# Attention stage of a fused layer kernel: the two layer-norm roots move from GpSimd into VectorE's Newton chain

## What is computed

```python
x = x + layernorm(attention(layernorm(x)))     # this stage; x is 32 x 256 x 128, fp32
# layernorm(x) = (x - mean) / sqrt(var + 1e-5), over the last axis
# attention:  Q, K = normalised 4-wide heads of xn @ Wq.T, xn @ Wk.T  (16 heads)
#             Qn = normalize(Q @ W_nudge);  V = xn @ Wv.T (64 per head)
#             scores = Qn.K * scale + k_bonus(K);  causal softmax;  out = P.V @ Wout.T
x = x + layernorm(ffn(layernorm(x)))           # later stages, not touched by the change
x = x + layernorm(recurrence(layernorm(x)))
x = x + layernorm(mixture_of_experts(layernorm(x)))
```

## Time and profile before

| | |
|---|---|
| median of 3 runs (lowest, highest) | 1899.07 us (1897.19, 1900.87) |
| the profiled execution | 1898.16 us, span 1896.4 us, mean granted TensorE clock 0.961 |
| PE busy over the span | 1695.4 us, 89% |
| PEld / DVE / ACT / POOL busy | 1240.9 / 1331.5 / 886.4 / 999.0 us (65 / 70 / 47 / 53%) |
| instructions | 43410 |
| the attention stage | from 0 to about 864 us of the span |

### The profile page before, as it was taken

How to read it: one execution, slowest core, us unless ns; L and a number is a source line. 1 busy time by engine, 2 the same in 40 slices (tenths; PEclk the granted TensorE clock), 3 DMA queues, 4 the chain that set the end, 5 groups by cost and what they waited for, 6 DMA issues and landing times. The chain is left out here.

```text
span 1896.4 us, 43410 instructions
## 1 busy us (share of the span) xinstructions
PE 1695.4 (89%) x12768; PEld 1240.9 (65%) x12768; DVE 1331.5 (70%) x4113; ACT 886.4 (47%) x1955; POOL 999.0 (53%) x1825
## 2 busy tenths in 40 slices
PE   4999999999999999975999999999999997568885
PEld 2666666666666666654778888888878885335553
DVE  6777777777777777753456777777777676457775
ACT  2655565555555555532344444444444442123332
POOL 6777766777777767742222333333333332137776
PEclk8999999999999999988999999999999998679997
DMA  1011111111110111201011000000010005034431
GB/s 39 10 52 40 36 50 50 50 50 50 50 44 31 50 50 50 78 12 39 12 56 56 29 29 29 29 32 31 31 36 32 27 23 196 33 109 121 127 115 36
DMA packets 78236, 95.72 MB, mean 50 GB/s; under 512 B 7046, under 2 KB 62995, under 8 KB 78160
## 3 DMA queue, kind: packets, MB, share of 16 engines
q1 hardware_dynamic: 70992, 77.91, 13.0%
q0 software_dynamic: 7168, 16.87, 2.5%
HBM read 53.14 MB, written 43.69 MB: 51 GB/s over the span
## 5 line engine op out<-in xcount | busy, mean ns | idle before, releaser
L648 ACT ACTIVATE wgu<-score 128x384 f32<-128x384 f32 x512 | 223.1, 489 | 99.8 <-PE score L472 94.5
L317 POOL TENSOR_SCALAR_AFFINE_SELECT wgu<-wgu 128x512 f32<-128x512 f32 x256 | 163.9, 640 | 155.1 <-ACT wgu L648 146.3
L1239 PE MATMUL main<-hT_high,h_high 128*128 128x512 f32 x512 | 223.5, 436 | 0.9 <-ACT hT_high L1448 0.9
L1241 PE MATMUL main<-hT_high,h_low 128*128 128x512 f32 x512 | 203.5, 398 | 0.0
L495 PE MATMUL outp<-wgu 128*64 128x256 f32 (+1 forms) x2048 | 197.8, 336 | 0.9 <-POOL wgu L317 0.9
L495 PEld LDWEIGHTS outp<-wgu 128*64 128x64 f32 x2048 | 128.5, 138 | 58.7 <-issue 17.8
L1248 PE MATMUL main<-hT_low,h_high 128*128 128x512 f32 x512 | 139.1, 393 | 0.1
L529 PE MATMUL back<-wout,wgu 128*128 128x128 f32 x1024 | 131.3, 282 | 0.0
L790 DVE TENSOR_TENSOR wgu<-spread,wgu 128x512 f32<-128x512 f32 x128 | 87.0, 680 | 61.9 <-PE spread L515 56.8
L1694 DVE SCALAR_TENSOR_TENSOR th<-th,main 128x512 f32<-128x512 f32 x64 | 43.9, 686 | 122.9 <-ACT th L1479 122.9
L1380 PE MATMUL main<-wgu,xgT 128*128 x192 | 106.0, 634 | 23.4 <-DVE xgT L1738 16.0
(11 more groups left out here) (270 smaller groups left out, 4205.3 us busy)
## 6 DMA issues: line engine op xcount, KB each, us to landing
sorted_d<-row_buf SPq DMA_DIRECT2D x26, 772.0 KB, 3.7
xg<-sorted_d SPq DMA_DIRECT2D x48, 386.0 KB, 3.2
wgu<-in_gate_up SPq DMA_DIRECT2D x4, 2048.0 KB, 9.0
xa<-in_x SPq DMA_DIRECT2D x32, 128.0 KB, 3.5
xr<-in_x SPq DMA_DIRECT2D x32, 128.0 KB, 3.2
x_d<-x SPq DMA_DIRECT2D x32, 128.0 KB, 1.9
x1c<-x_d SPq DMA_DIRECT2D x16, 256.0 KB, 2.8
x1v<-x_d SPq DMA_DIRECT2D x16, 256.0 KB, 2.7
```

The lines of the kernel that those rows point to most:

```text
L317: pool.affine_select(out=blocks, in_=blocks, compare_op=ALU.is_ge, fill=0.0, base=0, pattern=[[0, 4], [1, P]], channel_multiplier=-1).then ...
L648: act.activation(prob[:, h // 2 % (RING // 2), :, h % 2, :], score[h % BANKS][:, 0:SC].rearrange("p (c q) -> p c q", q=P), ACT.Exp).then_i ...
L1239: pe.matmul(main[m % 2][:, :], w[0][:, k, m * P:(m + 1) * P], src[0][:, k, :], start=(k == 0), stop=False)
L1241: pe.matmul(main[m % 2][:, :], w[1][:, k, m * P:(m + 1) * P], src[0][:, k, :], start=False, stop=False)
```

## The change

The GpSimd function `rstd` and its tiles are taken out. The tiles of the short Newton chain (ssg2, r2, nt2, nu2) grow from 32 to 36 columns; the last four hold the variances (two row tiles, for y and m) plus epsilon, times 0.25. A new DVE function `roots` waits for both sets of means and variances, writes these columns with one `tensor_scalar`, waits for that, and runs the chain, which gave the norm of the rotated q only and stood at the start of the next step. It is now at the end of the step, behind ssg2, and runs in each step that has an entry y or m, so in 37 steps where there were 32. `xn` is computed straight behind it, and `yn` and `x1` behind xn. In the PE step the wait for `rec` stands between the weighted values and the row totals of the first quarter and no longer ahead of both. The factor 0.25 with the chain's last factor 0.25 in place of 0.5 gives 1/sqrt(var + epsilon).

```diff
@@ -116,13 +116,10 @@
         back_row = sb("back_row", [P, HEADS])
         low_row = sb("low_row", [P, HEADS])
         low_sel = sb("low_sel", [P, 1])
-        pow_half = sb("pow_half", [P, 2, TT])
 
         xa = sb("xa", [P, TT, D])
         stat_a = sb("stat_a", [P, TT, 6])
         mv_ya = sb("mv_ya", [P, 2, TT, 2])
-        ve_ya = sb("ve_ya", [P, 2, TT])
-        rstd_ya = sb("rstd_ya", [P, 2, TT])
         xn = sb("xn", [P, TT, D])
         xnT = [sb(f"xnT{i}", [P, T]) for i in range(2)]
         sq1 = sb("sq1", [P, TT * 2 * HEADS, DH])
@@ -135,10 +132,11 @@
         qkT = sb("qkT", [P, T])
         sq2 = sb("sq2", [P, TT, HEADS, DH])
         ss2 = sb("ss2", [P, TT, HEADS])
-        ssg2 = sb("ssg2", [P, TT, HEADS])
-        r2 = [sb(f"r2_{i}", [P, TT, HEADS]) for i in range(4)]
-        nt2 = sb("nt2", [P, TT, HEADS])
-        nu2 = sb("nu2", [P, TT, HEADS])
+        NQ = TT * HEADS
+        ssg2 = sb("ssg2", [P, NQ + 2 * TT])
+        r2 = [sb(f"r2_{i}", [P, NQ + 2 * TT]) for i in range(4)]
+        nt2 = sb("nt2", [P, NQ + 2 * TT])
+        nu2 = sb("nu2", [P, NQ + 2 * TT])
         qraw = sb("qraw", [P, TT, HEADS, DH])
         ek = sb("ek", [P, TT, HEADS, DH])
         ek1 = sb("ek1", [P, TT, HEADS, DH])
@@ -282,7 +280,7 @@
             const(pool.memset(ident[:], 0.0))
             const(pool.affine_select(out=ident[:], in_=ident[:], compare_op=ALU.not_equal, fill=1.0, base=0,
                                      pattern=[[-1, P]], channel_multiplier=1))
-            const(pool.memset(pow_half[:], -0.5))
+            const(pool.memset(ssg2[:], 1.0))
             const(pool.tensor_copy(ident_b[:], ident[:]))
 
             def late_constants():
@@ -332,18 +330,6 @@
                         c += 1
                         wait_apart(pool, s[name], STEPS_K * n + c, s["const"])
                         v = rest[k + (2 if name == "qsplit" else 0)][:]
-
-            def rstd(y, m):
-
-                n = m if m is not None else y + 5
-                if y is not None:
-                    wait_apart(pool, s["mv_y"], TT * (y + 1), s["const"])
-                if m is not None:
-                    wait_apart(pool, s["mv_a"], TT * (m + 1), s["const"])
-                h = slice(0 if y is not None else 1, 2 if m is not None else 1)
-                pool.tensor_scalar(ve_ya[:, h], mv_ya[:, h, :, 1], 1.0, EPS, ALU.mult, ALU.add).then_inc(s["ve"], 1)
-                wait_apart(pool, s["ve"], n + 1, s["const"])
-                pool.tensor_tensor(rstd_ya[:, h], ve_ya[:, h], pow_half[:, h], ALU.pow).then_inc(s["rstd"], 1)
 
             def bonus(n, between):
 
@@ -444,8 +430,6 @@
                                            1.0, 0.0, ALU.mult, ALU.add)
                     pool.tensor_scalar(q_aug[:, :, 24:27], qp[:, :, :, DH], 1.0, 0.0,
                                        ALU.mult, ALU.add).then_inc(s["qaug"], 1)
-                if y is not None or m is not None:
-                    rstd(y, m)
                 mask(b, 7)
 
             rounds(pool, step)
@@ -480,7 +464,6 @@
                     return
                 if g == 0:
                     wait(pe, s["val"], 4 * (b + 1))
-                    wait(pe, s["rec"], b)
                 wait(pe, s["masked"], PAIRS_A * b + 2 * g + 2)
                 wait(pe, s["raw"], GROUPS * b + g)
 
@@ -496,6 +479,8 @@
                                           weights(h, k), start=(k == 0), stop=(k == 1),
                                           tile_position=(0, DV * i), skip_group_check=True)
                 m.then_inc(s["p_out"], 1)
+                if g == 0:
+                    wait(pe, s["rec"], b)
                 for k in range(2):
                     for j in range(GH):
                         m = pe.matmul(total[AUG * j:AUG * (j + 1), k * P:T], pick[:, g, :],
@@ -751,6 +736,19 @@
                     did(dve.scalar_tensor_tensor(out=r[k + 1][:], in0=nu[:], scalar=3 * w, in1=r[k][:],
                                                  op0=ALU.add, op1=ALU.mult))
 
+            def roots(y, m):
+
+                c = m if m is not None else y + 5
+                if y is not None:
+                    dve.wait_ge(s["mv_y"], TT * (y + 1))
+                if m is not None:
+                    dve.wait_ge(s["mv_a"], TT * (m + 1))
+                h = slice(0 if y is not None else 1, 2 if m is not None else 1)
+                both = ssg2[:, NQ:NQ + 2 * TT].rearrange("p (h i) -> p h i", h=2)
+                dve.tensor_scalar(both[:, h], mv_ya[:, h, :, 1], EPS, 0.25, ALU.add, ALU.mult).then_inc(s["ve"], 1)
+                dve.wait_ge(s["ve"], c + 1)
+                rsqrt(ssg2, r2, nt2, nu2, "rsq2", c, 0.25)
+
             def constants():
                 dve.wait_ge(s["w"], 96)
                 dve.tensor_copy(wv_part[0][:], wv[:]).then_inc(s["wv_split"], 1)
@@ -801,11 +799,10 @@
 
             def step(b, f, n, m, z, y, par):
                 if f is not None:
-                    rsqrt(ssg2, r2, nt2, nu2, "rsq2", f, 0.25)
                     wait(dve, s["qsplit"], STEPS_K * f)
                     wait(dve, s["qraw"], f + 1)
                     dve.tensor_tensor(q5[:, :, :, 0:DH], qraw[:],
-                                      r2[3][:].rearrange("p i (h o) -> p i h o", o=1)
+                                      r2[3][:, 0:NQ].rearrange("p (i h o) -> p i h o", i=TT, o=1)
                                       .to_broadcast([P, TT, HEADS, DH]), ALU.mult).then_inc(s["q4"], 1)
                 reciprocal(z)
                 last = isinstance(b, int) and b == B - 1
@@ -876,25 +873,25 @@
                     dve.wait_ge(s["ek1"], n + 1)
                     dve.reciprocal(sg[:], ek1[:]).then_inc(s["sg"], 1)
                     dve.wait_ge(s["ss2"], n + 1)
-                    dve.tensor_scalar(ssg2[:], ss2[:], NORM_MIN2, None, ALU.max).then_inc(s["ssg2"], 1)
+                    dve.tensor_scalar(ssg2[:, 0:NQ], ss2[:].rearrange("p i h -> p (i h)"), NORM_MIN2, None,
+                                      ALU.max).then_inc(s["ssg2"], 1)
                     dve.wait_ge(s["ssg2"], n + 1)
+                roots(y, m)
+                if m is not None:
+                    wait(dve, s["p_xnT"], m)
+                    for i in range(TT):
+                        mm = dve.tensor_scalar(xn[:, i, :], xa[:, i, :], mv_ya[:, 1, i, 0:1],
+                                               r2[3][:, NQ + TT + i:NQ + TT + i + 1], ALU.subtract, ALU.mult)
+                    mm.then_inc(s["xn"], 1)
                 if y is not None:
-                    wait(dve, s["rstd"], y + 6)
                     for i in range(TT):
                         mm = dve.tensor_scalar(yn[:, i, :], y_sb[:, i * D:(i + 1) * D], mv_ya[:, 0, i, 0:1],
-                                               rstd_ya[:, 0, i:i + 1], ALU.subtract, ALU.mult)
+                                               r2[3][:, NQ + i:NQ + i + 1], ALU.subtract, ALU.mult)
                     mm.then_inc(s["yn"], 1)
                     dve.wait_ge(s["yn"], y + 1)
                     wait(dve, s["xr"], 16 * (y + 1))
                     wait(dve, s["x1_out"], 16 * y)
                     dve.tensor_tensor(x1[:], yn[:], xr[:], ALU.add).then_inc(s["x1"], 1)
-                if m is not None:
-                    wait(dve, s["rstd"], m + 1)
-                    wait(dve, s["p_xnT"], m)
-                    for i in range(TT):
-                        mm = dve.tensor_scalar(xn[:, i, :], xa[:, i, :], mv_ya[:, 1, i, 0:1],
-                                               rstd_ya[:, 1, i:i + 1], ALU.subtract, ALU.mult)
-                    mm.then_inc(s["xn"], 1)
 
             rounds(dve, step)
 
```

More of the change, by code:

```diff
@@ L190, in attention_layer @@
         back = ps("back", [P, 512])
-        names = ("w", "const", "xa", "stat_a", "mv_a", "ve", "rstd", "xn", "p_xnT", "xnT", "p_qk", "sq1", "ss1",
+        names = ("w", "const", "xa", "stat_a", "mv_a", "ve", "xn", "p_xnT", "xnT", "p_qk", "sq1", "ss1",
                  "ssg1", "rsq1", "qkn", "p_qkT", "qkT", "p_rot", "sq2", "ek", "qraw", "ss2", "ssg2", "rsq2", "ek1",
```

## The result

The changed kernel takes 1907.1 us (median of 8 runs, 1902.51 to 1911.98), the kernel before in the same comparison 1899.05 (8 runs, 1897.14 to 1901.65): ratio 1.0041, 95% interval 1.0024 to 1.0058. The change costs 8 us. The forecast was 1898.6 with a range up to 1907.0, so it was too low by 8.5, and the median lies 0.1 above the range. The profiled execution took 1906.67 us (span 1904.9) against 1898.16 (span 1896.4).

What follows compares the result with a forecast made beforehand. PE was taken as the bound, waiting 0.88 us a step for xn. Loop -5.4 and pipeline ends +4.9 gave -0.5: 1897.7 from the profiled 1898.16, and 1898.6 as the median 0.9 above; range 1885 to 1907.

Steps and rivals of the forecast that it cites:

- The bound and what one step is worth: Attention loop: PE is the bound; its transpose of xn waits 0.88 us a step, 23.8 in 27 steps, the most recoverable.
- The walk through POOL's rows: DVE's chain beside POOL's instructions in the loop: 3.6 us long, xn earlier by 0.2 us a step, -5.4 in 27 steps.
- the xn pair: xn's two DVE instructions behind the chain in the loop: with POOL idle they take 0.60 us and not 1.00.
- ACT's copy held by yn: Loop: ACT's y_sb copy waits 1.4 us for yn; POOL's 1.44 us wait covers it: nothing, at most 0.3 a step.
- The ends: Both ends of the pipeline, where the chain is dearer than POOL's power: +4.9 us, bounds +3 and +7.
- (a) to (c): Pipeline start: second xn net +1.9 us, third xn about +0.7, PE's start behind ssg2 in the third step +0.65.
- The first xn: Start of the pipeline: the first root (entry 0) is hidden by the weights' load, so it costs nothing.
- (e): Pipeline's end: the last yn waits 2.7 us for its root, hidden by nothing, where it waited 1.09 for POOL: +1.6.
- The sum: Loop -5.4 and ends +4.9 make -0.5 us, so 1898.6; own range 1892 to 1905, chance 0.48.
- its own undoing: Prediction is wrong if POOL's instructions stand elsewhere in the step than put, or the ends cost more than 7 us.
- B: Rival: POOL holds the loop's chain throughout, 3.92 us; +1 to +12, with the ends 1905 to 1916; chance 0.20.
- C: Rival: ACT's copy waiting for yn becomes the new wait, delaying masks 0.3 us a step, +8, about 1907; chance 0.07.

## Why the prediction was wrong

- **The bound and what one step is worth: right.** PE's 0.88 a step was the most to be had, and with POOL waiting nearly all of it came: 0.8 us were left of 23.8.
- **The walk through POOL's rows: right.** Chain 3.6 forecast, 3.54 measured; held by the mask and both bonus instructions, as put; the xn pair 0.60 forecast, 0.60 measured. The fourth instruction passed the copy of k. The gain per step came out at 0.30 and not 0.2, since xn follows the chain by 0.03 and not by 0.15 and the chain is 0.06 shorter. -8.1 in place of -5.4, inside its bounds.
- **ACT's copy held by yn: right in kind, cost not quite nothing.** ACT waits 1.57 (forecast 1.4), and the cover of 1.44 at POOL is used up: PE waits 0.10 a step for masks, inside the bound of 0.3. It is why PE's wait fell by 0.43 and the step only by 0.30.
- **The ends: priced too low at the start.** The run with POOL's power there agrees with the 4.9 (4 to 6 measured), but even that run is 1.8 us behind before when the loop begins. In the changed kernel's own trace the pipeline's fill costs 6.6 where (a) to (c) made 3.3, and with the last root the ends cost 8.0, above the upper bound of 7: PE waits for the second xn 7.12 and not 3.35, for the third 0.81 and the fourth 1.29 where before had none:

```profile
27.31 0.69 PE L549 MATMUL front<-ident,xn 128*128 128x128 f32 x2 [7.12 <-DVE xn L883]
...
43.86 0.69 PE L549 MATMUL front<-ident,xn 128*128 128x128 f32 x2 [0.81 <-DVE xn L883]
...
66.52 0.69 PE L549 MATMUL front<-ident,xn 128*128 128x128 f32 x2 [1.29 <-DVE xn L883]
```

  The first xn, put at nothing, is 2.2 us later too (8.32 against 6.16), though that is down to 1.0 at the matmuls behind it. At the other end (e) was right: ACT's last y_sb is 1.90 earlier (856.59 against 858.49) and yn 0.46, so the root costs 1.4 (forecast 1.6).
- **The sum: right for what it summed, and in part by luck.** 6.6 at the start, -8.1 in the loop, -0.4 in the unrolled steps behind it and 1.4 for the last root make -0.5 at the last yn, which is what the trace shows (-0.46). The forecast has the same -0.5 because two misses cancel: the ends 3.1 dearer, the loop 2.7 better and 0.4 behind it. With the loop at its old place the changed kernel runs at 0.9992 of before (0.9983 to 1.0001), and -0.5 us is 0.9997.
- **The step that failed: the sum stops where the attention stage stops, and all code behind it was put at nothing without a reason.** It counts what each instruction costs where it runs, and not what 67 more of them do to the place of the code behind. That term is +8, more than all others leave together. Of what the prediction named as its own undoing, POOL stands in the step where it was put; the ends did come out above 7, but the loop paid for that. Nor was it one of the rivals: B's and C's times cover 1907 by chance, and the traces show 0.45 a step left and 0.10 for the masks.
- **The clock at the start of the next stage** is a small second term, not forecast. In the windows of 880 to 885 us before stands at a granted clock of 1.00 and the kernel after at 0.50:

```profile
880.00:885.00 5.00, 1.87 (x7) 1.25 (x8) 3.61 (x6) 1.57 (x3) 0.00 (x0) 1.00 0.00 0
```

```profile
880.00:885.00 5.00, 2.97 (x7) 1.86 (x7) 2.91 (x6) 1.21 (x2) 0.00 (x0) 0.50 0.00 0
```

  PE had no work from 860 to 870 in both. The rise comes some 11 us later after the change, and PE goes from 1.3 us ahead (872) to 0.6 behind (886), in the profiled run. Between runs of the changed kernel this varies: those with a mean clock of 0.962 took 1902.5 to 1903.9, those at 0.955 took 1910.3 to 1912.0. The loop's 8 us stand in the profiled runs beside it, so the two add.

## What to carry to other kernels

This is shown for one loop of one engine. When a change adds or removes instructions on an engine ahead of a hardware loop, look in the new trace at idle time without a releaser on the loop's first instruction, and at instruction packets in its passes; if both are new, put a few dozen instructions more ahead of it before judging the change. The price of this chain of small DVE instructions on the critical path was set by what POOL did beside it (3.54 us, and 2.67 with POOL standing): here a wait that made POOL stand for 2.5 us a step, off its own critical path, was worth 15 us (1884.45 against 1899.76). What an edit saves in a loop is set off by what the same edit costs in the unrolled steps at both ends, so both are summed.

## What the runs showed of the hardware that was not expected

- This loop of 352 instructions on DVE is read again at each pass behind the first or stays, by its place modulo 128: it stays at the six places tried from 68 to 100 and is read at 64, at 110 and at five places between them through 0. Each pass that is read (about five packets of 8 KB on q14) costs DVE 1.7 to 2.3 us ahead of its first instruction with data and PE 2.5 to 3.2, about 8 us in this kernel for three passes; at 64 DVE stands another 1.0 to 1.3 and PE loses 3.6 to 3.8 a pass.
- Seven instructions more left the loop in place (1901.4 against 1901.2) and twenty-nine made it be read again (ratio 1.0085).
- Waits that are already fulfilled cost DVE 0.10 us for each instruction of two (5.12 us for 52, 7.41 for 76).
- The granted clock at the start of the next stage rose from 0.50 to 1.00 at 888 us in the changed kernel and at 877 in the one before, without a change of the code there.
